# The second expert product of a mixture-of-experts layer turned round, on one Trainium2 core

## The reference, cut to what matters

```python
logits = jnp.einsum('btd,ed->bte', h, w_r) + b_r
topk_vals, topk_idx = jax.lax.top_k(logits, K)          # K = 2 of 8 experts
gates = jax.nn.softmax(topk_vals, axis=-1)
hid = jax.nn.gelu(jnp.einsum('nd,edf->nef', hf, W1) + b1, approximate=False)
expert_stack = jnp.einsum('nef,efd->ned', hid, W2) + b2
...
mixed = jnp.sum(gathered * gates_flat[:, :, None], axis=1).reshape(B, T, d)
return x + mixed
```

## Time and profile before

| | us |
|---|---|
| median of 3 runs (lowest to highest) | 105.89 (105.58 to 107.15) |
| the profiled execution: its own time | 105.69 |
| its span, first to last instruction | 104.0 |
| PE busy (435 matmuls) | 85.4, 82% of the span |
| PE loading weights | 67.6 |
| DVE busy | 58.5 |
| ACT busy | 55.4 |
| POOL busy | 32.5 |

### The profile page before, as it was taken

How to read it: one execution, slowest core, us unless ns; L and a number is a source line. 1 busy time by engine, 2 the same in 40 slices (tenths; PEclk the granted TensorE clock), 3 DMA queues, 4 the chain that set the end, 5 groups by cost and what they waited for, 6 DMA issues and landing times.

```text
span 104.0 us, 1441 instructions
## 1 busy us (share of the span) xinstructions
PE 85.4 (82%) x435; PEld 67.6 (65%) x435; DVE 58.5 (56%) x174; ACT 55.4 (53%) x120; POOL 32.5 (31%) x65
## 2 busy tenths in 40 slices
PE   0081998499699995379999999999999999989940
PEld 0051437467499983369777777777777776779940
DVE  0998569688989555628809113404041329259870
ACT  0757814689998412213934564645556563118750
POOL 6963130039999624400000005415050505000000
PEclk9999999999999999955569999999999999999999
DMA  0589999090000000000000000000000000003774
GB/s 5 67 294 403 323 290 276 21 378 28 0 9 0 0 0 0 0 0 0 0 0 0 6 0 0 0 0 0 0 0 0 6 0 0 0 3 106 297 275 129
DMA packets 8168, 7.59 MB, mean 73 GB/s; under 512 B 1441, under 2 KB 6241, under 8 KB 8033
## 3 DMA queue, kind: packets, MB, share of 16 engines
q1 hardware_dynamic: 7440, 7.41, 22.5%
q10 hardware_dynamic: 720, 0.10, 0.6%
HBM read 5.40 MB, written 2.11 MB: 72 GB/s over the span
## 4 chain that ended last, share of the span: by engine, by line
PE 70%; DVE 15%; ACT 4%; issue 4%; DMA 3%; POOL 1%; DVEq 0%
PE ps L1214 20%; PE ps L1133 8%; PE ps L1299 7%; PE ps L1203 6%; PE ps L1204 6%; PE ps L1205 5%; PE ps L1047 4%; PE ps L1092 3%; DMA ends_i<-in_end_ids 3%; DVE closest L842 2%; PE ps L1226 1%; ACT hn_t L573 1%; PE ps L1107 1%; PE ps L1118 1%; ACT L638 1%
## 5 line engine op out<-in xcount | busy, mean ns | idle before, releaser
L657 ACT ACTIVATE w_f<-ps,ffn_cols 128x384 f32<-128x384 f32 x32 | 18.2, 580 | 15.9 <-PE ps L1205 15.9
L1214 PE MATMUL ps<-w_f 128*128 128x384 f32 x64 | 26.0, 496 | 0.0
L1203 PE MATMUL ps<-hn_hi,w_hi 128*128 128x384 f32 (+2 forms) x35 | 21.4, 613 | 1.4 <-DVE hn_lo L888 1.2
L513 POOL TENSOR_TENSOR acc<-acc,term 128x384 f32<-128x384 f32 x6 | 8.6, 1439 | 34.3 <-DVE term L973 34.3
L973 DVE SCALAR_TENSOR_TENSOR term<-ps,ffn_cols,gate_bc 128x384 f32<-128x384 f32 (+2 forms) x9 | 5.1, 571 | 22.8 <-PE ps L1214 15.9
L1204 PE MATMUL ps<-hn_lo,w_hi 128*128 128x384 f32 (+2 forms) x35 | 12.8, 366 | 0.0
L1205 PE MATMUL ps<-hn_hi,w_lo 128*128 128x384 f32 (+2 forms) x35 | 12.7, 364 | 0.0
L1214 PEld LDWEIGHTS ps<-w_f 128*128 128x128 f32 x64 | 11.8, 193 | 0.9
L1203 PEld LDWEIGHTS ps<-hn_hi,w_hi 128*128 128x128 f32 x35 | 7.8, 222 | 5.8 <-DVE hn_lo L888 1.3
L1204 PEld LDWEIGHTS ps<-hn_lo,w_hi 128*128 128x128 f32 x35 | 7.9, 227 | 3.8 <-issue 0.3
L461 POOL TENSOR_TENSOR w_lo<-w_f,w_hi 128x512 fp32r<-128x512 f32 x8 | 10.0, 1276 | 0.0
(11 more groups left out here) (185 smaller groups left out, 134.1 us busy)
## 6 DMA issues: line engine op xcount, KB each, us to landing
w_f<-in_w SPq DMA_DIRECT2D x4, 512.0 KB, 7.0
w_f<-in_w SPq DMA_DIRECT2D x8, 256.0 KB, 6.9
out_y<-w_f SPq DMA_DIRECT2D x6, 256.0 KB, 2.6
cls_all<-cls_dram SPq DMA_DIRECT2D x1, 1024.0 KB, 4.3
out_y<-w_f SPq DMA_DIRECT2D x4, 128.0 KB, 2.3
wm_sb<-in_wm ACTq DMA_DIRECT2D x1, 64.0 KB, 2.4
emb<-in_weight SPq DMA_DIRECT2D x1, 32.0 KB, 2.8
ffn_cols<-in_ffn_columns ACTq DMA_DIRECT2D x1, 24.0 KB, 5.2
```

What stands on the lines that cost most here:

```text
L513: G.tensor_tensor(acc[:], acc[:], term[:, e % 2], ALU.add).then_inc(acc_ready, 1)
L657: nc.scalar.activation(hid[:, e % 2, f], ps[:, n % 4, 0:ROWS], ACT.Gelu, bias=b1_col[:, e, f:f + 1]).then_inc(gelu_ready, 1)
L1203: M(dst, w1_hi[:, e, c], hn_hi[:, rows], start=True, stop=False)
L1214: M(ps[:, 4 + e % 2, 0:ROWS], w2_f[:, e, f], hid[:, e % 2, f], start=(f == 0), stop=(f == FT - 1)).then_inc(down_done, 1)
```

## The change

`down` is turned round: the 128 x 128 block of `hid` for one row tile and one hidden block is stationary and the block of `W2` streams, 128 columns. The result has rows on partitions. `down(e, i)` makes one row tile of one expert in four matmuls (8 passes) and needs all four gelus of the expert at its first tile; three of them stand for one expert, behind `up(e + 1, 0)`, `up(e + 1, 1)` and `up(e + 1, 2)`. The results go round the four banks 4 to 7, and a `down` waits for the `weigh` of the tile four before.

A gate is now a value per partition, read from `gate` by a DVE instruction as a scalar. `weigh(e, i)` multiplies and adds to `acc` (rows on partitions) in one instruction; the bias is added ahead of that in 24 instructions `weigh_bias`, from `b2_rows`, the second bias on every partition, loaded by SP. Gone are `turn_gates`, the split of the gates, `pick`, `gates`, ACT's copies, `turn_base`, POOL's adds and the summing stage on PE. The table is made from `acc` tile by tile, and the first seven groups of the final loop wait for two tiles of it. The banks of the final loop are counted from 0 in place of 3.

The diff, cut to its core:

```diff
-        ffn_cols = sb("ffn_cols", [P, 2 * E + E * FT])
-        wr_t, b2_col = ffn_cols[:, 0:E], ffn_cols[:, E:2 * E]
+        ffn_cols = sb("ffn_cols", [P, E + E * FT])
+        b2_rows = sb("b2_rows", [P, E, D])
...
+            sp.dma_start(b2_rows[:].rearrange("p e d -> p (e d)"), b2.to_broadcast([P, E * D])).then_inc(b2_in, 16)
+
             sp.wait_ge(clsrow_ready, 1)
...
-            for e in range(E - 2):
-                sum_up(e)
...
-                        act.wait_ge(down_done, n - 2 * FT + 1)
+                        act.wait_ge(down_done, NT * (e - 1))
                     nc.scalar.activation(hid[:, e % 2, f], ps[:, n % 4, 0:ROWS], ACT.Gelu,
                                          bias=b1_col[:, e, f:f + 1]).then_inc(gelu_ready, 1)
-                    if e == 2 and f == 0:
...
-                        take_gates(e - 2)
-            take_gates(E - 2)
-            take_gates(E - 1)
...
-                V.tensor_tensor(base[:, i], h1[:, i], w_ln[:, i], ALU.add).then_inc(base_ready, 1)
+                V.tensor_tensor(acc[:, i], h1[:, i], w_ln[:, i], ALU.add).then_inc(acc_step, 1)
...
+            step(V.tensor_tensor(gate[:], chosen[:], grec[:].to_broadcast([P, NT, E]), ALU.mult))
+
+            def weigh_bias(e, i):
+
+                dve.wait_ge(acc_step, NT * (e + 1))
+                V.scalar_tensor_tensor(out=acc[:, i], in0=b2_rows[:, e], scalar=gate[:, i, e:e + 1], in1=acc[:, i],
+                                       op0=ALU.mult, op1=ALU.add).then_inc(acc_step, 1)
+
+            def weigh(e, i):
+
+                m = e * NT + i
+                dve.wait_ge(down_done, m + 1)
+                if e >= 1:
+                    dve.wait_ge(weighed, m - NT + 1)
+                V.scalar_tensor_tensor(out=acc[:, i], in0=ps[:, 4 + m % 4, 0:D], scalar=gate[:, i, e:e + 1],
+                                       in1=acc[:, i], op0=ALU.mult, op1=ALU.add).then_inc(weighed, 1)
+
+            def make_table(i):
+                dve.wait_ge(weighed, NT * (E - 1) + i + 1)
+                V.tensor_copy(tab[:, i, 0], acc[:, i]).then_inc(table_ready, 1)
+                dve.wait_ge(table_ready, 2 * i + 1)
+                V.tensor_tensor(tab[:, i, 1], acc[:, i], tab[:, i, 0].bitcast(F32), ALU.subtract).then_inc(table_ready, 1)
...
             class_ids()
             settle()
-            for e in range(2, E):
-                one_hot(e - 2)
-                weigh(e - 2)
...
+            dve.wait_ge(b2_in, 16)
+            for e in range(E):
+                for i in range(NT):
+                    weigh_bias(e, i)
+            dve.wait_ge(acc_step, NT * (E + 1))
+            for e in range(E - 1):
+                for i in range(NT):
+                    weigh(e, i)
+                one_hot(e)
             one_hot(HOT_STEPS - 1)
...
+            for i in range(NT):
+                weigh(E - 1, i)
+                make_table(i)
...
-            def down(e, f):
-                if f == 0:
+            def down(e, i):
+
+                m = e * NT + i
+                if i == 0:
                     pe.wait_ge(w2_in[e // 2], 32)
...
-                pe.wait_ge(gelu_ready, FT * e + f + 1)
-                M(ps[:, 4 + e % 2, 0:ROWS], w2_f[:, e, f], hid[:, e % 2, f], start=(f == 0),
-                  stop=(f == FT - 1)).then_inc(down_done, 1)
...
+                    if e == 0:
+
+                        pe.wait_ge(logit_read, NT)
+                    pe.wait_ge(gelu_ready, FT * (e + 1))
+                if m >= 4:
+
+                    pe.wait_ge(weighed, m - 3)
+                for f in range(FT):
+                    mm = M(ps[:, 4 + m % 4, 0:D], hid[:, e % 2, f, tile(i)], w2_f[:, e, f], start=(f == 0), stop=(f == FT - 1))
+                mm.then_inc(down_done, 1)
...
             for e in range(1, E):
                 for f in range(FT):
                     up(e, f).then_inc(up_done, 1)
-                    if e == 1 and f == 1:
-                        turn_gates()
...
-                    down(e - 1, f)
-            for f in range(FT):
-                down(E - 1, f)
-                if f == 1:
-                    gates(E - 1)
+                    if f < NT:
+                        down(e - 1, f)
+            for i in range(NT):
+                down(E - 1, i)
...
-            for n, tiles in enumerate(((0, 1), (2,))):
-                pe.wait_ge(term_ready, E - 1)
...
-                mm.then_inc(mixed_done, 1)
...
-                pe.wait_ge(table_ready, 2 if g < 7 else 4)
+                pe.wait_ge(table_ready, 4 if g < 7 else 6)
```

More of the change, by code:

```diff
@@ L56, with build @@
 UNITS = NT * PAIRS
-GR = LOW + E
 HT = 2 * B
-def build(nc, x, weight, end_ids, columns, wv, wm, b_r, w1, ffn_columns, w2, out):
+def build(nc, x, weight, end_ids, columns, wv, wm, b_r, w1, ffn_columns, b2, w2, out):
     ctx = ExitStack()
@@ L193, in build @@
         grec = sb("grec", [P, NT, 1])
[L195 to L201, removed]
+        gate = sb("gate", [P, NT, E])
+        acc = sb("acc", [P, NT, D])
         tab = sb("tab", [P, NT, 2, D], F32R)
@@ L1239, in _ @@
                 up(0, f, late_rows if f < FT - 1 else slice(0, ROWS)).then_inc(up_done, 1)
[L1241 to L1252, removed]
             for e in range(1, E):
@@ L1256, in _ @@
                     up(e, f).then_inc(up_done, 1)
-                    if e == 1 and f == 1:
-                        turn_gates()
-                    if e == 2 and f == 0:
-                        turn_base()
-                    if e >= 2 and f == (2 if e == 2 else 0):
-                        gates(e - 2)
-                    if e == E - 1 and f == FT - 1:
-                        gates(E - 2)
-                    down(e - 1, f)
-            for f in range(FT):
-                down(E - 1, f)
-                if f == 1:
-                    gates(E - 1)
-            pe.wait_ge(gelu_ready, E * FT)
-            for n, tiles in enumerate(((0, 1), (2,))):
-                pe.wait_ge(term_ready, E - 1)
-                for i in tiles:
-                    M(ps[:, i, 0:D], term[:, E % 2, i * P:(i + 1) * P], ident[:], start=True, stop=False)
-                pe.wait_ge(acc_ready, E - 2)
-                for i in tiles:
-                    M(ps[:, i, 0:D], acc[:, i * P:(i + 1) * P], ident[:], start=False, stop=False)
-                pe.wait_ge(term_ready, E + n)
-                for i in tiles:
-                    mm = M(ps[:, i, 0:D], term[:, (E - 1) % 2, i * P:(i + 1) * P], ident[:], start=False, stop=True)
-                mm.then_inc(mixed_done, 1)
+                    if f < NT:
+                        down(e - 1, f)
+            for i in range(NT):
+                down(E - 1, i)
+            pe.wait_ge(gelu_ready, E * FT)
             pe.wait_ge(hot_out, HOT_STEPS)
@@ L1317 @@
         "w1": pre["L0_ffn_W1"],
-        "ffn_columns": np.concatenate([pre["L0_ffn_w_r"].T, pre["L0_ffn_b2"].T,
-                                       pre["L0_ffn_b1"].reshape(E * FT, P).T], 1),
+        "ffn_columns": np.concatenate([pre["L0_ffn_w_r"].T, pre["L0_ffn_b1"].reshape(E * FT, P).T], 1),
+        "b2": pre["L0_ffn_b2"].reshape(1, E * D),
         "w2": pre["L0_ffn_W2"],
```

75 lines of the change are left out of this document (9 added, 66 removed).

## The result

| | before | after |
|---|---|---|
| median (lowest to highest), 20 runs each | 105.9 us (105.21 to 107.24) | 106.84 us (106.07 to 107.91) |
| the profiled execution: its own time | 105.69 | 106.49 |
| its span | 104.0 | 104.8 |
| mean granted clock in it | 0.951 | 0.935 |

The ratio of after to before is 1.0079, with a 95% interval of 1.0044 to 1.0113: slower by about 0.8%, a real difference, though under the 2% that was set as the bound. The ratio leaves out runs that lie more than 1.5% above the fastest of their kernel.

The account below looks back on a forecast made before the run. The prediction took PE to bound the expert stage, other engines counting only where PE waits. From 105.69 us, 1.63 (late clock, first stretch) + 2.23 (second stretch) - 2.17 (third stretch) gave 107.4 us, range 105.0 to 109.0.

Parts of the forecast that it names:

- gates and summing stage: Gates' matmuls gone from the second stretch, 1.4 us saved; summing matmuls gone from the tail, which saves 2.17 us.
- the second stretch: From expert 1's first `down` to the end of the last: 33.70 us against 31.47, 2.23 longer.
- The prices: PE passes at full clock: 0.1117 us for 128 columns, 0.323 for 384; a row tile of `down` 0.89 us.
- The new wait: PE waits for the youngest gelu ahead of first tiles: 0.41 us at experts 1 to 6, 0.93 at expert 7.
- the hand-over: From the end of ACT's gelu to PE's next instruction: 0.05 us taken, 0.15 as the upper bound.
- the first stretch: From 51.90 us to expert 1's first `down`: 0.07 us late with the early clock, 1.63 with the late one.
- The third stretch: Last PE pass to the final matmul: 0.40 us in place of 2.57, which saves 2.17.
- DVE: 24 bias products ahead of the first `weigh`, 0.83 us a round, 6.6 in all; costs PE nothing to 0.5 us.
- The late clock: At the expert stage's start the clock rises at 57.3 us, not 54.0, costing 1.63 us; the forecast, chance 0.47.
- its cases of 54.0 (0.07) and 55.6 (about 0.85): Earlier clock rises at the stage's start: at 54.0 the first stretch is 0.07 us late; 55.6 gives 106.6 us.
- rival 1: At the stage's start the clock rises at 54.0 as before: 105.8 us, not slower; chance 0.28.
- The rule from the Trainium skill: Basis of rival 3: the clock falls again at the steady stage's waits, costing 8.2 us, 115.6 in all; chance 0.03.

Follow-up runs that it names:

- e1: The changed kernel with the row tiles of all experts one `up` later on PE; 103.45 us, ratio to the kernel before 0.977.
- e5: The changed kernel with only two experts' bias products ahead of the first `weigh`, the others behind a `weigh` each; 106.47 us, ratio to before 1.0031.
- e4: The changed kernel with two extra wide PE passes, results unused, filling the break ahead of expert 0's first tile; 106.33 us, ratio to before 1.0054.
- e2: The changed kernel with only expert 0's row tiles one `up` later on PE; 106.63 us, ratio to before 1.0055.
- e10: The changed kernel with 17 wide filling passes in PE's idle moments between 40 and 51 us; 105.36 us, ratio to before 0.996.
- e11: The kernel before with 17 wide filling passes in PE's idle moments between 40 and 51 us; 103.43 us, ratio to before 0.9776.
- e8: e1 with DVE's bias products spread behind `weigh`s and its last one-hot steps earlier; 102.62 us, ratio to before 0.9676.
- e9: e8 with 17 wide filling passes in PE's idle moments between 40 and 51 us; 99.95 us, ratio to before 0.9472.

## Why the prediction was right, point by point

- *A little slower, inside 2%.* Forecast 107.4, range 105.0 to 109.0; measured 106.84. The order of the terms held: gates and summing stage won, waits lost more. The size is not that of the sum: it had 1.69 more than the profiled execution before, and 0.80 were measured between the two profiled executions. The clock's term came out 1.15 lower (0.48 in place of 1.63), the second stretch 0.34 higher, and PE reached the stage 0.12 earlier.
- *The prices.* A row tile takes 0.89 us at full clock as forecast, and the turned product itself costs nearly nothing. e1 shows it from the other side: with the waits gone the turned product is 2.4 us faster than the kernel before.
- *The new wait.* Forecast 0.41 and 0.93, measured 0.46 and 0.95 (0.88 of standing and 0.07 in the passes). The term that was mis-sized is the hand-over: from the gelu's end to the load it took 0.11 (58.47 to 58.58) and 0.07 (89.79 to 89.86) in place of 0.05, and the first pass follows 0.03 to 0.04 behind the load. With it, and the load of expert 1's first weights, which the forecast had in the first stretch, the second stretch is 2.57 longer, where 2.23 was the forecast.
- *The third stretch.* Forecast 0.40 from the last pass to the final loop, measured 0.39.
- *DVE.* The bias products took 0.91 us a round (7.27 for eight), the upper bound, not the 0.83 taken. The first `weigh` came at 59.62 in place of about 59.15, PE waited for it by less than 0.1 us, and e5 gained 0.1 at most.
- *The late clock.* This step was too large, and its reason isn't borne out. It took one moment for the rise before (54.0) and one after (57.3), 1.6 us dearer; no run shows the 3.2 us that it counted afresh from the end of the first tile, and the latest rise in any trace is at 55.6. In the profiled execution it rose at 54.8, and the first stretch grew by 0.48, which is what the forecast's own arithmetic gives for such a rise, half-way between its cases of 54.0 (0.07) and 55.6 (about 0.85). That the sum ended near the measured time although this term was over three times too large in that execution is luck in part.
- *What the clock did over many runs.* They show a mixture: in the high group the changed kernel takes 106.13 (5 of 20 runs), in the low one 107.17; the kernel before takes 105.84 (20 of the 29 runs beside e1 to e4) and 106.84. So at like clock the change costs 0.3, which is rival 1 (0.1 forecast), and the step between the groups is 1.0, not 1.6. The rest of the 0.9 is that fewer runs of the changed kernel are in the high group. How far the change does that isn't shown: the kernel before had 20 of 29, 9 of 19, 5 of 7 and 8 of 17 runs there from one series to the next, and of the 20 timed beside the change, whose clock isn't on record, 11 lie at 105.9 and under and 9 at 106.39 and over. That the break does it is not shown either: e4 speaks for it, e1 and e2 against it, and in the traces the rise goes with the fall, which comes well ahead of the break. Whether the 128-column passes after the break have a part in it, as the forecast argued, was not tried.
- *What rival 1 left out.* The 0.3 holds for a stage that starts at half clock. With the filling passes (e10 against e11) the change costs 1.9: the kernel before gains 2.6 from them, the changed one 1.5. PE stands 0.8 us ahead of its first tile there (49.90 to 50.71), where it was 0.3 (51.78 to 52.09).
- *The rule from the Trainium skill* ("TensorE: Matmul & The Clock Gate", "A second HAM failure mode: psum-queue depth-cycling"), a clock that swings with short idle moments between groups of matmuls: in the steady stage the clock stayed at 2.4 GHz through six breaks of 0.46 us, so it didn't apply there. At the stage's start, behind 1.3 us of idle time, e10's profiled execution shows a second stop of 0.65 us going with a fall; by their mean clock, four of its 12 runs had the stop without the fall.

## What to carry to other kernels

When an operand changes from streaming to stationary, ask which instruction now needs all of it, and what work lies between its producer and that instruction: here one step of shift in a hand-written order was worth 3.4 us, over three times what the change lost. Then look for the engine that is late next, in this case DVE, with bias products at the front and one-hot steps at the tail. And a break in PE's work ahead of a long stage can cost the clock too, as in e10's profiled execution; whether it does is read from several executions, with the fall of the clock beside its rise, before one run's rise is laid to the break.

## What was not expected of the hardware

The clock's rise lay at 54.0, 54.8, 55.0 and 55.6 us in the profiled executions of the kernel before, of the changed kernel, e1 and e2. In the ten kernels without filling passes ahead of the stage it came 10.2 to 10.3 us after the fall in four and 13.6 to 13.7 us after it in six, with kernels that have the break in both groups. And runs of one kernel fall into groups a microsecond apart; a single profile doesn't tell which one a median stands in. The idle moments of PE ahead of the expert stage are worth more than all that the change touched: 17 passes whose results nobody reads made e8 2.7 us faster (e9) and the kernel before 2.6 us (e11 against 106.05 beside it).
